# A GRU recurrence that places its input product and bias in PSUM from ScalarE and VectorE instead of by TensorE

## The reference

```python
def cell(h, x):
    gi = x @ W_ih + b_ih
    gh = h @ W_hh + b_hh
    i_r, i_z, i_n = jnp.split(gi, 3, axis=-1)
    h_r, h_z, h_n = jnp.split(gh, 3, axis=-1)
    r = sigmoid(i_r + h_r)
    z = sigmoid(i_z + h_z)
    n = tanh(i_n + r * h_n)
    return (1.0 - z) * n + z * h
hs = lax.scan(cell, initial_state, inputs)      # 128 steps, 16 rows
logits = hs @ Wg + bg                           # top 2 of 4 experts, softmax
for i in range(4):                              # 512 tokens for each expert
    h = gelu(tok @ W1[i]); out[sel] += (h @ W2[i]) * p
return x + out
```

## Time and profile before

| | us |
|---|---|
| median of 3 runs (836.11 to 837.08) | 836.3 |
| the profiled execution's own time | 836.27 |
| its span, first to last instruction | 834.5 |
| TensorE busy in the span | 803.0 |
| VectorE busy | 619.8 |
| ScalarE busy | 421.1 |
| GpSimd busy | 179.9 |

### The profile page before, as it was taken

The page is one execution under the profiler, slowest core; times in us unless marked ns, Lnnn a source line. Parts: engine busy times, 40 slices in busy tenths (PEclk is TensorE's granted clock), DMA queues, the critical chain, the costliest instruction groups (busy, mean ns, idle before and its releaser), DMA issues.

```text
span 834.5 us, 28320 instructions
## 1 busy us (share of the span) xinstructions
PE 803.0 (96%) x11781; PEld 528.0 (63%) x11782; DVE 619.8 (74%) x2113; ACT 421.1 (50%) x885; POOL 179.9 (22%) x459
## 2 busy tenths in 40 slices
PE   7999999999999999999995799999999999999996
PEld 3446556679999999999994444454445444444442
DVE  6979899878888888888888879767666676755300
ACT  0677666645566556554455448252835184417400
POOL 1002222123433334333330010121012101210011
PEclk9999999999999999999997899999999999999998
DMA  9810000000111010000001943471347224630022
GB/s 336 323 48 2 2 2 3 2 3 4 54 60 50 17 42 5 4 4 5 5 4 33 269 156 119 135 226 27 113 139 194 57 101 151 171 81 1 1 26 26
DMA packets 24286, 62.64 MB, mean 75 GB/s; under 512 B 4386, under 2 KB 4386, under 8 KB 22308
## 3 DMA queue, kind: packets, MB, share of 16 engines
q1 hardware_dynamic: 19312, 51.42, 18.1%
q0 software_dynamic: 3584, 8.42, 5.5%
q10 hardware_dynamic: 1268, 1.08, 0.4%
HBM read 52.50 MB, written 12.62 MB: 78 GB/s over the span
## 4 chain that ended last, share of the span: by engine, by line
PE 92%; DVE 5%; issue 1%; DMA 1%; ACT 0%; POOLq 0%; DVEq 0%
PE ps L459 29%; PE ps L666 20%; PE ps L680 20%; PE ps L451 10%; PE ps L469 3%; PE ps L434 3%; PE ps L424 2%; PE ps L600 1%; PE ps L653 1%; DVE big L1541 1%; PE ps L472 1%; DMA wa<-in_x_t 1%; DVE halves L1264 1%; DVE wa L1253 1%; PE ps L644 0%
## 5 line engine op out<-in xcount | busy, mean ns | idle before, releaser
L459 PE MATMUL ps<-halves,wa 128*128 128x64 f16 x8448 | 289.1, 193 | 1.4 <-DVE halves L1264 1.2
L459 PEld LDWEIGHTS ps<-halves,wa 128*128 128x128 f16 x8448 | 271.2, 98 | 20.2 <-DVE halves L1264 4.2
L680 PE MATMUL ps<-big 128*128 128x512 f16 x768 | 166.9, 379 | 0.0
L666 PE MATMUL ps<-hx,big 128*128 128x512 f16 x768 | 166.9, 379 | 0.0
L779 ACT ACTIVATE wa<-ps,un_gates 128x128 f32<-128x128 f32 x288 | 100.1, 365 | 111.0 <-PE ps L459 100.6
L680 PEld LDWEIGHTS ps<-big 128*128 128x128 f16 x768 | 75.1, 98 | 89.9
L666 PEld LDWEIGHTS ps<-hx,big 128*128 128x128 f16 x768 | 74.8, 98 | 90.0 <-issue 0.2
L784 ACT ACTIVATE wa<-wa,un_gates 128x64 f32<-128x64 f32 x288 | 97.4, 344 | 53.0 <-DVE wa L1253 48.9
L451 PE MATMUL ps<-hx,wb 128*128 128x512 f16 x432 | 106.9, 379 | 1.2 <-issue 1.1
L861 ACT ACTIVATE hx<-ps,un_hid_in 128x512 f32<-128x512 f32 x64 | 43.6, 682 | 109.2 <-PE ps L666 106.9
L1264 DVE SCALAR_TENSOR_TENSOR halves<-ocand,neg_scale,wa 128x64 f16<-128x64 f32 (+1 forms) x288 | 80.6, 280 | 4.4 <-issue 0.5
(11 more groups left out here) (221 smaller groups left out, 791.4 us busy)
## 6 DMA issues: line engine op xcount, KB each, us to landing
wa<-in_w SPq DMA_DIRECT2D x28, 1024.0 KB, 5.2
hs_rows<-big SPq DMA_DIRECT2D x8, 512.0 KB, 6.3
big<-in_w_hh SPq DMA_DIRECT2D x4, 768.0 KB, 19.6
wb<-in_w SPq DMA_DIRECT2D x12, 256.0 KB, 2.6
big<-in_w_ih SPq DMA_DIRECT2D x2, 1024.0 KB, 12.5
hx<-in_x_t SPq DMA_DIRECT2D x2, 1024.0 KB, 16.5
big<-in_w_ih ACTq DMA_DIRECT2D x2, 512.0 KB, 6.6
wa<-in_x_t SPq DMA_DIRECT2D x2, 512.0 KB, 6.2
```

Of the source, the lines that this page charges most:

```text
L459: mm = pe.matmul(gate_ps[:, j, g, :], whh_parts[:, k, w, (4 * g + j) * P:(4 * g + j + 1) * P], halves[:, src, k, h, :], start=False, stop= ...
L666: mm = pe.matmul(ps[:, m % 2, :], w1p[:, w, k, m * P:(m + 1) * P], tokT[:, t, k, :], start=(k == 0 and n == 0), stop=(k == KD - 1 and n == 2))
L680: mm = pe.matmul(ps[:, 2 + g % 2, :], hid[:, h, k, g * P:(g + 1) * P], w2p[:, w, k, :], start=(k == 0 and n == 0), stop=(k == KH - 1 and n ...
```

## The change

The input product is stored once, in 32 bits, and no matmul adds it any more. Instead another engine writes scale times input product (128 columns for the gates r and z) and the bias b_hn (64 columns for gate n) straight into the PSUM bank, and the 144 matmuls accumulate on top. I call such a pair of writes a **seed**.

- Up to step 23 the seeds of the next step are written by VectorE at the end of its step, eight operations (`seed_next`), and TensorE waits for `seeded_early`.
- From step 24 on ScalarE writes them, after the eighth activation of its step (`seed_ahead`): units 0 to 2 for the step after the next, in two operations (`seed_most`, 384 and 192 columns, into the other one of two sets of three banks), and unit 3 for the next step, in two operations (`seed_last`, 128 and 64 columns; unit 3 has one bank). TensorE waits for `seeded` at its first matmul and for `last_seeded` at the first matmul of unit 3.
- All low halves are made by VectorE; states and low halves of units 0 to 2 are one operation each (192 columns). In an exact step `one_less_z` of unit 2 comes ahead of `candidate_in` of unit 3.
- `ORDER` is another table. Its last seven entries are unit 3's, and one entry of unit 3 stands fifth.
- In rough steps `fill` runs as one block of 18 ahead of the gates, and the gates run unit by unit.
- The splits `rz_high`, `rz_low` and the preparation of b_hn for a matmul (`split_bhn`) are gone.

```diff
-        INJECT = 2
-        ORDER = ((INJECT, 0, 0), (INJECT, 1, 0), (HIGH, 1, 0), (INJECT, 2, 0), (HIGH, 0, 0), (HIGH, 2, 0),
-                 (INJECT, 3, 0), (HIGH, 0, 1), (HIGH, 1, 1), (LOW, 1, 0), (HIGH, 2, 1), (LOW, 2, 0),
...
+        ORDER = ((HIGH, 2, 0), (HIGH, 1, 0), (HIGH, 0, 0), (HIGH, 2, 1), (HIGH, 3, 1), (HIGH, 0, 1),
+                 (HIGH, 2, 2), (HIGH, 0, 2), (HIGH, 1, 2), (HIGH, 1, 1), (LOW, 0, 0), (LOW, 0, 1), (LOW, 0, 2),
+                 (HIGH, 0, 3), (HIGH, 1, 3), (LOW, 0, 3), (LOW, 1, 0), (LOW, 1, 1), (LOW, 1, 2), (LOW, 1, 3),
+                 (HIGH, 2, 3), (LOW, 2, 2), (LOW, 2, 3), (LOW, 2, 0), (LOW, 2, 1), (HIGH, 3, 0), (LOW, 3, 0),
+                 (HIGH, 3, 2), (LOW, 3, 1), (HIGH, 3, 3), (LOW, 3, 2), (LOW, 3, 3))
...
-        POOL_LOWS = LOW_BY.count("P")
...
             def gates_rough(src, i):
...
+                fill(filled(i), filled(i + 1))
+                for j in range(KD):
+                    pe.wait_ge(S["seeded_early"], 2 * (KD * i + j + 1))
+                    for k in range(KD):
+                        pe.wait_ge(S["high_ready"], made(i) + k + 1)
+                        unit(0, HIGH, j, k, src, (HIGH,), k == KD - 1)
...
+                    if j not in begun:
+                        begun.add(j)
+                        if early:
+                            pe.wait_ge(S["seeded_early"], 2 * (2 * half_steps + j + 1))
+                        elif j == KD - 1:
+                            pe.wait_ge(S["last_seeded"], half_steps + (2 - 2 * FILLED))
+                        elif j == ORDER[0][1]:
+                            pe.wait_ge(S["seeded"], half_steps + (2 - 2 * FILLED))
...
+            def seed_most(bank, rows_of, before):
+
+                act.wait_ge(S["rn_done"], before)
+                act.activation(gate_banks[bank][:, :, 0:2 * COLS], rows_of(slice(0, KD - 1)), ACT.Copy,
+                               scale=seed_s[:, 0:1]).then_inc(S["seeded"], 1)
+                act.activation(gate_banks[bank][:, :, 2 * COLS:GATES],
+                               bhn_s[:, 0:KD - 1].unsqueeze(2).to_broadcast([P, KD - 1, COLS]), ACT.Copy
+                               ).then_inc(S["seeded"], 1)
...
+            def seed_ahead(i):
+
+                if i + 2 < FIRST + L:
+                    seed_most(bank_of(i + 2), rows_at(i + 2), KD * (i + 2))
+                if i + 1 < FIRST + L:
+                    seed_last(rows_at(i + 1), KD * (i + 2))
...
             for i in range(FIRST + L):
-                step(KD * i)
+                step(KD * i, bank_of(i))
+                if i >= FILLED:
+                    seed_ahead(i)
...
+            def seed(i, j):
+
+                c = (i // STEPS_C + CHUNK_ORDER[0]) % NC_
+                dve.tensor_scalar(gates_of(0, j)[:, 0:2 * COLS], gi_rz[:, c, j, i % STEPS_C, :], seed_s[:, 0:1], None,
+                                  ALU.mult).then_inc(S["seeded_early"], 1)
+                dve.tensor_copy(gates_of(0, j)[:, 2 * COLS:GATES], bhn_s[:, j:j + 1].to_broadcast([P, COLS])
+                                ).then_inc(S["seeded_early"], 1)
...
-                         (one_less_z, 0), (candidate_in, 2), (blend, 0), (keep_state, 0), (one_less_z, 1),
-                         (reset, 3), (blend, 1), (candidate_in, 3), (one_less_z, 2), (keep_state, 1), (blend, 2),
-                         (one_less_z, 3), (keep_state, 2), (blend, 3), (keep_state, 3), (low_part, 2),
-                         (low_part, 3))
+                         (one_less_z, 0), (candidate_in, 2), (blend, 0), (one_less_z, 1), (reset, 3), (blend, 1),
+                         (one_less_z, 2), (candidate_in, 3), (blend, 2), (keep_state, most), (one_less_z, 3),
+                         (low_part, most), (blend, 3), (keep_state, last), (low_part, last),
+                         *((seed_next, j) for j in range(KD)))
```

More of the change, by code:

```diff
@@ L766, in _ @@
                 x_high(0, k)
-            for m in range(3, ACT_HIGHS):
+            for m in range(3, TILES_EARLY):
                 first_tile(m)
-                first_tile_high(m)
             act.wait_ge(S["gates_known"], 1)
@@ L1206, in whh_low @@
+            for j in range(KD):
+                seed(0, j)
             def whh_low(n):
@@ L1228, in w1_peak, with step @@
                 dve.tensor_reduce(peak[:, W1:W1 + 1], sq[:, :], AX.X, ALU.max).then_inc(S["w_peak"], 1)
-            def step(gi_n, after, src, base, low, moved=False, ahead=(), between=(), bias_added=True):
+            def step(gi_n, after, src, base, low, bank, moved=False, between=(), following=None):
                 dst = 1 - src
@@ L1337, in _ @@
                     after = lambda j, i=i: hs[:, j, i - FIRST + 1, :]
[L1338 to L1343 removed]
+                between = []
                 if 1 <= s <= KD and q < 2:
@@ L1351, in _ @@
                     between.append((w1_peak, 0))
-                step(lambda j, c=c, cols=cols: gi[:, c, j, 2, cols], after, i % 2, KD * i, i >= ROUGH - 1, moved, ahead, between,
-                     i >= ROUGH)
+                step(lambda j, c=c, cols=cols: gi[:, c, j, 2, cols], after, i % 2, KD * i, i >= ROUGH - 1, bank_of(i), moved,
+                     between, i + 1 if i + 1 < FILLED else None)
             def run(steps):
```

256 lines of the change are left out of this document (94 added, 162 removed).

## The result

The changed kernel takes **929.96 us** (median of 4 runs, 928.59 to 932.93), the kernel before 836.48: ratio 1.112, 95% interval 1.109 to 1.115, or 93.5 us more. 916 was predicted, with a range of 893 to 955. The profiled execution took 929.77 us, with a span of 928.0.

What follows compares the result with a forecast made beforehand. TensorE's own work was taken as the bound in all 72 steps. 836.3 - 4.0 (start and rough steps) + 4.9 (steps 20 to 24) + 78.8 (late steps) = 916 us; 893 to 955 should hold 8 of 10.

Steps and rivals of the forecast that it cites:

- Part 2: Late steps 24 to 71: TensorE waits for unit 3's seed, a loop of 6.7 us against 5.0 per step, +78.8 us.
- tanh 3 at +1.43: Late steps: unit 3's tanh starts 1.43 us after the start of unit 3's last matmul (t = 0), where it was.
- Rival (a): Late steps: TensorE's clock falls as well; +41 us if in every second step, 957 us in all; chance 20%.
- Part 3: Steps 20 to 24: VectorE writes the seeds behind its last low half, so TensorE waits; +4.9 us (+2 to +7).
- Part 4: Start and rough steps: -1.0 at the start, 4.5 us saved in rough steps with 1.5 given back; -4.0 us together.
- the tail: Everything after step 71: as before, no change.
- The start: Ahead of the first `fill`: the split of x has three `rz_low` less in front of it, -1.0 us.
- The lost injections: The 20 rough steps: one injection of 128 columns per unit goes from TensorE, 4.5 us saved.
- The price of a seed pair: VectorE's two writes that seed one unit take 0.40 us; four such pairs per rough step.
- VectorE's merged states and low halves cost or bring nothing: VectorE's merged operations, and GpSimd's two lost low halves, lie in the shade of the wait: no cost, no gain.
- Rival (b): Late steps: unit 3's seed is not late, the chain through unit 2 sets 4.87 us per step; 830 us; chance 5%.

Runs made afterwards that it cites:

- experiment 9: Changed kernel plus 11 extra 256-column TensorE matmuls per late step, in the wait for last_seeded: 916.2 us; the same matmuls behind that wait: 1010.4 us.
- experiment 4: Kernel before, with only VectorE's and GpSimd's lists as in the change (merged states and low halves, none on GpSimd): 873.1 us.
- experiment 7: experiment 3 plus the edits of experiment 5 and experiment 6 together: 827.2 us, ratio 0.989 to the kernel before.
- experiment 8: experiment 7 with VectorE's and GpSimd's lists of the kernel before, the merged operations taken apart again: 853.0 us.
- experiment 2: Changed kernel with seed_last issued between tanh 2 and tanh 3 in ScalarE's list, TensorE's order left alone: 844.6 us.
- experiment 3: experiment 2 plus a new order of TensorE's products, unit 3's first product sixth: 842.2 us.
- experiment 1: Changed kernel with one entry of ORDER moved: unit 3's first product goes from fifth place to the front of unit 3's own group: 850.8 us.
- experiment 6: experiment 3 with ScalarE, not VectorE, writing unit 3's seed behind tanh 3 in rough steps 1 to 19: 835.2 us.
- experiment 5: experiment 3 with ScalarE, not VectorE, writing the seeds in steps 20 to 23, and step 24's seed right after step 22's last tile: 833.8 us.

## Why the prediction was right, and where it was off

**Part 2, the wait that comes: right in mechanism, and near in size.** The releaser, the place (once per late step), the list ScalarE works through, and tanh 3 at +1.43 are as predicted. The seeds took 1.24 us instead of 1.42, so the period is 6.47 instead of 6.7, and the waits for L755 are 68.1 us in all where I had some 85. The terms, guessed from writes of other widths: 384 columns 0.565 (0.54 guessed), 192 columns 0.31 (0.41), 128 columns 0.35 (0.37), 64 columns 0.20 (0.34). The two that read one number per unit were guessed 0.14 and 0.10 too high, the other two within 0.03. The Trainium skill (ScalarE: Activation LUTs, "Step-by-step: what each stage is for") calls PSUM ScalarE's lower-latency destination. Whether that holds here these rows leave open: the 64-column copy took 0.20 against the 0.344 of the tanh of the earlier trace rows, the 128-column one 0.35 against the 0.365 of the sigmoid, and function and source differ too. The loop alone gives 304.1 - 236.06 = +68, which is 11 below my 78.8.

**Rival (a), the clock: it did happen, in its lighter form.** I held it apart from the forecast at 20%, as +41 for a fall in every second step; it came in nine steps of 47, +14. So in the late steps +82 against +78.8 hides two errors of opposite sign, -11 and +14; the other 11 us of the 14 between 916 and 930 are parts 3 and 4 and the tail. I called the rule that activity lifts the clock (TensorE: Matmul & The Clock Gate, "What's actually happening", in the Trainium skill) a question of how little TensorE does in a period; experiment 9 shows that reading to be wrong for this kernel.

**Part 3, steps 20 to 24: right in mechanism, half the size.** +10.3 against +4.9, beyond my range of +2 to +7; without the clock's share of 4.0 it is +6.3, inside it. The seeds started at +3.33 where I had +2.9, and the first matmul of step 23 at +4.71 where I had +4.15. To this come the clock (6.94 and 5.78 us for blocks of 4.36, +4.0), which I had left out here although its pause of 4.5 us is the longest of all steps, and waits of 1.2 and 0.3 us in steps 20 and 21 which I took to be hidden by `fill`.

**Part 4, start and rough steps: the term that failed.** I had -4.0 and measured +0.3. The start gave 1.4 us in the profiled execution (1.0 predicted), but this says little: in the ten traces that share the changed start, the first `fill` begins between 48.57 and 50.24, against 50.57 before. The lost injections were worth the 4.5 us that I had worked out: with VectorE's list relieved, the rough steps take 111.96 instead of 116.48. But "of the rough steps' 4.5 us I give 1.5 back" should have been 6.2. The price of a seed pair was right (0.40 predicted, 0.38 found). What I got wrong was VectorE's room: I read it from its busy share, 96.2 of 107.7 us, and let it be filled to the last. A good part of that idle time lies inside the chain of a step, where nothing else in a list of fixed order can go. In the change, where VectorE sets the pace of the rough steps, it is still idle for 6.9 of the 106.8 us from 58.2 to 165, and from 60 to 165 us 4.0 of its idle time stand right ahead of `blend`, which needs the result of the `one_less_z` just before it; in the kernel before it was 4.2.

**"VectorE's merged states and low halves cost or bring nothing"** was true only because the longer wait covered them. Alone they cost 37 us (experiment 4), and once the wait is gone the kernel of experiment 7, with its TensorE order, needs them (26 us, experiment 8).

**Rival (b), the faster one,** named the condition that it depends on, the seed written ahead of tanh 3. Experiment 2 made it so and got a period of 4.97 where I had worked out 4.87; with the order of experiment 3 it is 4.93. Its total of 830 assumed the late steps to be all that was wrong; with the two further repairs it is 827.

## What to carry to other kernels

When work moves from a full engine to one with idle time, look for the loop it closes: from the last reader of the buffer through the new writer's list to the first instruction that waits. Its length is a floor for the period whatever the engines' shares say, and it can be cut at either end, by the place in the writer's list or by the place of the first use. Measure an engine's room as the longest gap in its list at the place where the new work would stand, not as its idle share. And when a large wait has been found, price the next bound behind it too: here there were three, which the prediction had underpriced or put at nothing: the low halves, the seeds of steps 20 to 24 and VectorE's list in the rough steps; with all three in place the repaired late steps left the change 14 us slower than before (experiment 1), with none of them it is 9 us faster.

## What the hardware showed beyond what I expected

- TensorE's granted clock fell towards its lower level (rows of 0.50) in nine late steps of the change, with pauses of 1.46 us and 0.39 to 0.47 us and 0.7 us of work between them. In the kernel before it was 1.00 through one pause of 2.80 us behind full work and fell 1.4 us after it, among a few small matmuls. With the 1.46 us filled it stayed at the higher level; with 1.2 us more work behind the pause it fell more often. A fall cost 1.3 to 1.6 us in a late step.
- In step 23, which follows the longest pause of the steps, the block was slow in every run with a pause of 3.4 to 4.5 us (the change and experiments 1, 2, 3, 6 and 9: 5.5 to 6.9 us), and not with 1.70 or 2.03 us (experiments 5, 7 and 8: 4.36 us). In step 24, behind 2.4 to 2.55 us, it was slow in the change and in experiment 1 (5.78 and 5.79 us), and not in experiments 2, 3 and 6 (4.36 us). No run shows what decides there.
- GpSimd's 64-column product took longer where VectorE worked on 512 columns. In the rough steps of the change (one line, its durations in ns, minimum, median and maximum):

```profile
L959 POOL TENSOR_TENSOR wa<-wa,halves x76: 299/320/1027, 59.2 to 163.1; 128x64 f32<-128x64 f32 x76
```

  One that began at 149.66, beside VectorE's L1177 (149.64 to 150.39), took 892 ns, and one at 155.22, again beside L1177 (from 155.20), 0.89 us; the median is 320. In the kernel before such meetings were rarer: mean 316 from 80 to 160 us, and the longest, 750, in a group of three that began at 67.14, beside VectorE's L1211 of 512 columns (67.21 to 68.01). It cost nothing here, since `blend` of unit 0 began at 151.64 anyway. The Trainium skill (GPSIMD Engine Reference, 1. Specifications) says that the two engines share SBUF interfaces and contend where a VectorE instruction has two SBUF inputs, as L1177 has; the trace agrees for this 512-column operation.
- ScalarE's writes into PSUM grow with their width by 0.84 ns per column: 203, 310, 350 and 565 ns for 64, 192, 128 and 384 columns, where those of 64 and 192 columns read one number per unit and partition, and the other two read every column.
